# A Mamba layer with mixed inputs: sample mixing, step sizes and their series moved to other slots of a pass

## What is computed

```python
x = x + attn(cond(x, cond_128, ...))      # mixing of tokens, then a Mamba-2 layer
x = x + ffn(cond2(x, cond_128, ...))      # grouped convolution, then a gated dense layer

# cond: a small MLP on cond_128 gives 8 softmax weights per sample
agg_w = einsum('bk,koi->boi', att, weight); out = einsum('boi,bih->boh', agg_w, x) + agg_b
# attn: projection to gate, x, B, C and dt
conv = silu(causal 4-tap convolution of x, B, C)
dt_p = softplus(dt + dt_bias); dA = exp(dt_p * -exp(A_log))
state = state * dA + (dt_p * x) B;  y = state C + D x    # over the 32 tokens of a sample
y = rms_norm_by_group(y) * norm_weight * silu(gate);  out = y @ out_proj.T
```

## Time and profile before

| | us |
|---|---|
| median of 3 runs | 1548.5 (1547.95 to 1549.09) |
| the profiled execution | 1547.9 |
| its span in the trace | 1546.1 |
| TensorE busy | 1516.0 (98%) |
| VectorE busy | 1114.8 (72%) |
| ScalarE busy | 751.2 (49%) |
| GpSimd busy | 656.7 (42%) |

### The profile page before, as it was taken

The page is one execution under the profiler, slowest core; times in us unless marked ns, Lnnn a source line. Parts: engine busy times, 40 slices in busy tenths (PEclk is TensorE's granted clock), DMA queues, the critical chain, the costliest instruction groups (busy, mean ns, idle before and its releaser), DMA issues. The chain is left out here.

```text
span 1546.1 us, 31966 instructions
## 1 busy us (share of the span) xinstructions
PE 1516.0 (98%) x12839; PEld 1243.0 (80%) x12839; DVE 1114.8 (72%) x1725; ACT 751.2 (49%) x1302; POOL 656.7 (42%) x687
## 2 busy tenths in 40 slices
PE   8999999999999999999999999999999999999997
PEld 6778888888888888888877888888888888888687
DVE  6877767767777777777877767777777767777567
ACT  4654445454454445454564544545454544544442
POOL 4443544435253544434343352544434352543406
PEclk9999999999999999999999999999999999999999
DMA  6120212122120212111023221112121121113212
GB/s 221 60 71 23 83 35 69 56 57 67 49 66 18 81 37 69 55 56 55 9 68 124 56 69 49 52 31 77 42 69 55 56 69 48 50 32 102 93 37 109
DMA packets 57843, 97.71 MB, mean 63 GB/s; under 512 B 9120, under 2 KB 17824, under 8 KB 57696
## 3 DMA queue, kind: packets, MB, share of 16 engines
q1 hardware_dynamic: 57696, 95.67, 20.7%
HBM read 86.73 MB, written 8.91 MB: 62 GB/s over the span
## 5 line engine op out<-in xcount | busy, mean ns | idle before, releaser
L462 PE MATMUL PS<-xh,wh 128*128 128x512 f32 x1280 | 520.6, 407 | 0.7 <-DVE xl L967 0.6
L1041 DVE SCALAR_TENSOR_TENSOR cb<-PS,P,cb 128x496 f32<-128x496 f32 (+2 forms) x576 | 412.7, 717 | 128.8 <-ACT cb L772 115.0
L462 PE MATMUL PS<-xh,wl 128*128 128x512 f32 x1280 | 502.7, 393 | 0.0
L462 PE MATMUL PS<-xl,wh 128*128 128x512 f32 x1280 | 502.5, 393 | 0.0
L1343 POOL TENSOR_TENSOR wl<-rw,wh 128x512 fp32r<-128x512 f32 x160 | 206.1, 1293 | 221.4 <-ACT wh L717 207.5
L1353 POOL TENSOR_TENSOR ysum<-yq 128x256 f32<-128x256 f32 x128 | 112.6, 879 | 418.4 <-ACT yq L812 417.0
L462 PEld LDWEIGHTS PS<-xh,wl 128*128 128x128 f32 x1280 | 241.7, 189 | 52.6
L462 PEld LDWEIGHTS PS<-xh,wh 128*128 128x128 f32 x1280 | 242.1, 189 | 51.8 <-issue 1.3
L462 PEld LDWEIGHTS PS<-xl,wh 128*128 128x128 f32 x1280 | 242.1, 189 | 45.5
L772 ACT ACTIVATE cb<-PS,P 128x512 f32<-128x512 f32 x192 | 148.2, 772 | 179.4 <-PE PS L462 179.3
L560 PE MATMUL PS<-oh,yh 128*128 128x512 f32 x512 | 200.2, 391 | 2.5 <-issue 0.9
(11 more groups left out here) (189 smaller groups left out, 1861.2 us busy)
## 6 DMA issues: line engine op xcount, KB each, us to landing
rw<-in_w_in SPq DMA_DIRECT2D x160, 256.0 KB, 2.7
ro<-in_w_out SPq DMA_DIRECT2D x64, 256.0 KB, 3.1
dab<-rates SPq DMA_DIRECT2D x128, 128.0 KB, 3.2
x2s<-acc SPq DMA_DIRECT2D x16, 256.0 KB, 3.0
out_x<-acc SPq DMA_DIRECT2D x16, 256.0 KB, 2.5
acc<-in_x SPq DMA_DIRECT2D x3, 1024.0 KB, 10.1
wh<-x2s SPq DMA_DIRECT2D x8, 256.0 KB, 3.7
wl<-x2s SPq DMA_DIRECT2D x8, 256.0 KB, 4.6
```

Of the source, the lines that this page charges most:

```text
L462: mm = e.matmul(PS[:, proj_bank(n, m), :], w[:, m, 128 * k:128 * k + 128], v[:, k, a:a + 512], start=(i == 0), stop=(i == 11))
L1041: e.scalar_tensor_tensor(out=cv[:, :, d:32], in0=pv[:, :, 0:32 - d], scalar=P[:, P_CW + 4 * c + 3 - d:P_CW + 4 * c + 4 - d], in1=cv[:, :, ...
```

## The change

Mixing moves to slots 1 to 4 and `dt_product` to slot 5, now in bank PT for every block; it waits for `dt_summed` of the block before instead of for `scale_turned`. `dt_lower`, `dt_summed` and `dt_first` move to slot 6. Of the series of blocks 1 to 3, steps 0 to 4 run in VectorE's slot 8, steps 5 to 7 in slot 9, steps 8 to 11 in slot 4 of the next pass. The operands for mixing are made a slot or more earlier, those of tile 4 in front of the first taps. The wait for `dt_turn` of the block before moves from `dt_lower` to step 1 of the series, which overwrites `dr`; `turn_x`, second half, waits for `dt_summed` of this block, and Y no longer does. In pass 0, `G_all` moves to slot 4 and `G_mask` and the filling of `diag` to slot 5, `context` to slot 6, `side_inputs` to slot 9, GpSimd's mixing weights for tiles 12 to 15 from slot 4 to slot 3; `decays(0)` waits for `context`, since its output lies over that product's operand.

```diff
@@ -197,7 +197,7 @@
             return (SEG[0], PT, PY[1], PY[0])[i] if n == END else PO[i]
 
         def D_bank(b):
-            return PY[0] if b else PT
+            return PT
 
         def S_bank(n, i):
             return (PY[0] if i < 2 else SEG[0]) if n == END else PG
@@ -423,7 +423,7 @@
                 pe.wait_ge(wd_lo)
                 pe.wait_ge(x_lo, 4 * b + 3)
                 if b:
-                    pe.wait_ge(dtx_ok, ({1: 0, 2: 15, 3: 16}[b], 1))
+                    pe.wait_ge(d_sum, (b - 1, 1))
                 both = wds[:, :, :, :].rearrange("p k s c -> p k (s c)")
                 e.matmul(PS[:, D_bank(b), :], both[:, 0, :], xh[:, 0, a:a + 512], start=True, stop=False)
                 for k in range(4):
@@ -472,13 +472,11 @@
                     else:
                         pe.wait_ge(acc_ok, (n - 1, 3))
                 else:
-                    if n == 0:
-                        pe.wait_ge(d_sum, (0, 1))
-                    else:
+                    if n:
                         pe.wait_ge(dtx_ok, (n - 1, 3))
                         pe.wait_ge(acc_ok, (n - 1, 1))
-                    if n in BLOCK_AT and n >= 1:
-                        pe.wait_ge(x_lo, 4 * BLOCK_AT[n] + 3)
+                    if n in BLOCK_AT:
+                        pe.wait_ge(d_sum, (BLOCK_AT[n], 1))
                     if n in TURNED:
                         pe.wait_ge(dt_ok, TURNED[n])
                 for i in (0, 1):
@@ -510,8 +508,6 @@
                     pe.wait_ge(y_ok, (n, 1))
                 if i == 0:
                     pe.wait_ge(dtx_ok, (n, 1))
-                    if n in BLOCK_AT:
-                        pe.wait_ge(d_sum, (BLOCK_AT[n], 1))
                     if n >= 1:
                         pe.wait_ge(acc_ok, (n - 1, 3))
                     else:
@@ -576,25 +572,25 @@
                         dt_product(0)
                     if m == 6 and n in TURNED:
                         dt_turn(TURNED[n], n)
-                    if b is not None and 2 <= m <= 5:
-                        mix_tile(4 * b + m - 2, n)
-                    if m == 2:
-                        if n:
-                            Y(n - 1, 2)
-                            Y(n - 1, 3)
+                    if b is not None and 1 <= m <= 4:
+                        mix_tile(4 * b + m - 1, n)
+                    if n and m == 2:
+                        Y(n - 1, 2)
+                        Y(n - 1, 3)
+                    if m == (2 if n else 4):
                         G_all(n)
-                    if n == 0 and m == 5:
+                    if n == 0 and m == 6:
                         context()
                     if n and m in (1, 3, 4, 5):
                         i = (1, 3, 4, 5).index(m)
                         O(n - 1, i)
                         if i != 1:
                             S(n - 1, {0: (0,), 2: (1, 2), 3: (3,)}[i])
+                    if m == 5 and b is not None:
+                        dt_product(b)
                     if m == 7:
                         turn_x(n, 0)
                         turn_x(n, 1)
-                    if m == 8 and b is not None:
-                        dt_product(b)
                     if m == 9:
                         Y(n, 0)
                         Y(n, 1)
@@ -731,7 +727,6 @@
             def dt_lower(b):
                 act.wait_ge(D_ok, b)
                 if b >= 1:
-                    act.wait_ge(DT_ok, b - 1)
                     act.wait_ge(rate_out[b - 1], 1)
                 else:
                     act.wait_ge(mix, 2)
@@ -829,7 +824,7 @@
                         y_square(n - 1, 3)
                     if n == 0 and m == 1:
                         dt_lower(0)
-                    if b is not None and m == 9:
+                    if b is not None and m == 6:
                         dt_lower(b)
                     if m == 2:
                         silu(n, 1)
@@ -838,8 +833,6 @@
                     evac(n, m)
                     if n == 0 and m == 1:
                         dt_first(0)
-                    if b is not None and m == 9:
-                        dt_first(b)
                     if m == 6 and n in TURNED:
                         dt_turned(TURNED[n])
                     if n == 0 and m < 6:
@@ -848,6 +841,8 @@
                         silu(n, m - 1)
                     if n and m == 3:
                         y_high(n - 1, 3)
+                    if b is not None and m == 6:
+                        dt_first(b)
                     if m == 6:
                         scale_x(n, 0)
                         scale_x(n, 1)
@@ -857,8 +852,8 @@
                         split_o_hi(n // 2, m - 5)
                     if n % 2 == 1 and n < END:
                         split_w_hi(n // 2 + 1, m)
-                    if b is not None and 2 <= m <= 5:
-                        mixed_hi(4 * b + m - 2)
+                    if b is not None and 1 <= m <= 4:
+                        mixed_hi(4 * b + m - 1)
 
             def x3_biased(T):
                 act.wait_ge(conv_ok, T // 4)
@@ -996,6 +991,8 @@
                         if k == 11:
                             dve.wait_ge(rate_in, 1)
                         dve.wait_ge(d_step, (b, k - 1))
+                        if k == 1 and b:
+                            dve.wait_ge(DT_ok, b - 1)
                         if k == 1:
                             op = e.reciprocal(dr[:, :], da[:, :])
                         elif k == 2:
@@ -1021,6 +1018,7 @@
                 dve.wait_ge(ld_rate, n)
                 if n == 0:
                     dve.wait_ge(diag_ok)
+                    dve.wait_ge(cx_pe)
                 e.tensor_tensor_scan(Lt[:, :], dab[:, :], diag[:, :], 0.0, ALU.mult, ALU.max).then_inc(L_ok.sem, 1)
 
             def split_o_lo(u, j):
@@ -1115,18 +1113,19 @@
                 for m in range(10):
                     if n == 0 and m == 1:
                         dt_summed(0)
+                    if n == 0 and m == 0:
+                        mix_operands(4)
                     if n == 0 and m < 6:
                         taps(0, m)
                     if n == 0 and m == 0:
-                        mix_operands(4)
                         mix_operands(5)
                         mix_operands(6)
                     if n == 0 and m == 2:
                         mix_operands(7)
-                    if n >= 1 and n + 1 in BLOCK_AT and m in (6, 7):
-                        mix_operands(4 * BLOCK_AT[n + 1] + m - 6)
-                    if n and b is not None and m in (2, 4):
-                        mix_operands(4 * b + 1 + m // 2)
+                    if n >= 1 and n + 1 in BLOCK_AT and m in (6, 7, 9):
+                        mix_operands(4 * BLOCK_AT[n + 1] + {6: 0, 7: 1, 9: 2}[m])
+                    if n and b is not None and m == 3:
+                        mix_operands(4 * b + 3)
                     if n:
                         if m in (2, 5, 6):
                             variance(n - 1, {2: (0,), 5: (1, 2), 6: (3,)}[m])
@@ -1149,10 +1148,11 @@
                             add_out(n - 1, 2)
                         if m == 6:
                             add_out(n - 1, 3)
-                    elif m == 3:
+                    elif m == 5:
                         G_mask(n)
-                    if n == 0 and m == 6:
+                    if n == 0 and m == 9:
                         side_inputs()
+                    if n == 0 and m == 5:
                         e.tensor_copy(diag[:, :].rearrange("p (a t) -> p a t", a=32),
                                       bc(C[:, C_EQ:C_EQ + 32].rearrange("p (a t) -> p a t", a=1), 128, 32, 32)).then_inc(diag_ok.sem, 1)
                     if m == 7:
@@ -1162,18 +1162,20 @@
                         scale_turned(n, 1)
                         decayed(n, 0)
                         decayed(n, 1)
-                    if b is not None and m == 9:
+                    if b is not None and m == 6:
                         dt_summed(b)
                     if n and m < 6:
                         taps(n, m)
                     if n % 2 == 0 and m >= 6:
                         split_o_lo(n // 2, m - 6)
-                    if b is not None and 2 <= m <= 5:
-                        mixed_lo(4 * b + m - 2)
+                    if b is not None and 1 <= m <= 4:
+                        mixed_lo(4 * b + m - 1)
                     if n == 0 and 1 <= m <= 3:
                         dt_series(0, 4 * m - 4, 4 * m)
+                    if b is not None and m in (8, 9):
+                        dt_series(b, *((0, 5), (5, 8))[m - 8])
                     if n - 1 in BLOCK_AT and m == 4:
-                        dt_series(BLOCK_AT[n - 1], 0, 12)
+                        dt_series(BLOCK_AT[n - 1], 8, 12)
 
             def x3_low(T):
                 dve.wait_ge(x3_hi, T)
@@ -1385,12 +1387,12 @@
                         first_rates(TURNED[n])
                     if n == 0 and m < 6:
                         split_w_lo(0, m + 4)
```

(4 more changed lines are left out.)

## The result

The changed kernel takes 1555.2 us (median of 20 runs, 1553.7 to 1556.5) against 1549.5 for the kernel before in the same session: a ratio of 1.0039 (95% interval 1.0033 to 1.0046), 6.0 us slower by this ratio and 5.8 by the medians. The forecast was +2.1 us, 1550.6: right in sign, but inside what a measurement could tell from no change, and nearly 4 us short.

What follows compares the result with a forecast made beforehand. TensorE, busy 98%, bounds the kernel; only its waits and low clock, 21 us, can be won. Terms -9.9 - 2.1 + 6.5 + 4.7 + 2.9 = +2.1 us on 1548.5 gave 1550.6, range 1542.5 to 1555.5.

Steps and rivals of the forecast that it cites:

- term 3 of the series' end: Pass 0: GpSimd holding VectorE delays the first series by +1.7 us, between -3.8 and +4.4; series end forecast at 51.3.
- the mixing in pass 16: Pass 16: mixing one slot earlier puts each `mix_tile` closer behind its `mixed_lo`; cost taken as 0, at most 0.70 us.
- the first two: Pass 0, series end: one more `mixed_lo` less the mask, +0.3 us; idle time before `mixed_lo(4)`, +2.15 us.
- the −9.9: Passes 1 and 17: S waits (4.5 us), their low clock (3.4) and Y waits (2.0) all go.
- an earlier load: Passes 1 and 17: the scan of decays gets its load some 5 us earlier, so the Y waits (2.0 us) go.
- The O waits: New waits for late `y_out` and `y_low`: pass 1 +3.1 us plus 1.6 clock, pass 17 +2.1 plus 0.8.
- `dt_first` in front of the split: Before pass 17: `dt_first` with table load, 2.5 us in ScalarE's slot 6, delays `split_o_hi(8,1)`, then `decayed` and `y_out`.
- Pass 15, taken at nothing: Pass 15: steps moved to slots 8 and 9 cost 0; no output weights split, TensorE has 2 us of slack.
- The wait of `dt_product(3)` and the old O wait: Pass 16: both waits vanish, -1.2 us by the new bank and -0.9 by moving `dt_first` to slot 6.
- (a): Rival, faster: moved steps fit beside TensorE's last two projections, no O wait comes; -5.5 us, 1543.0; chance 0.23.
- (c): Rival, neutral: pass 0 costs little, series end near 49.5, O waits as forecast; +0.3 us, 1548.8; chance 0.13.
- (b): Rival, slower: GpSimd holding at +4.4 in pass 0, full low clock in pass 17; 1554.1 us; chance 0.22.

Runs made afterwards that it cites:

- pool_slot4: Changed kernel with GpSimd's mixing weights for tiles 12 to 15 back from slot 3 to slot 4; ratio 1.0013 to the kernel before.
- tile4_behind: Changed kernel with the operands of tile 4 made behind the first taps again; ratio 1.003 to the kernel before, median 1555.4 us.
- three_mended: Changed kernel with pool_slot4 and tile4_behind, plus series steps 0 to 2 in slot 8 and 3 to 11 in the next slot 4; ratio 0.999.
- passes_15_16_3_9: Kernel before with the change in passes 15 to 17 alone, series steps 0 to 2 in slot 8, 3 to 11 in slot 4; ratio 0.998.
- first_late: Changed kernel with `dt_first` behind `split_o_hi` in ScalarE's slot 6 instead of in front; ratio 1.0044 to the kernel before.
- pass_0: Kernel before with the change in pass 0 and for block 1 alone, passes 15 to 17 as before; ratio 1.0054.
- series_slot4: Changed kernel with all twelve series steps of blocks 1 to 3 back in slot 4 of the next pass; ratio 1.0046 to the kernel before.
- before_rates_first: Kernel before with `dab`'s load in front of the load of weights in SyncE's queue, nothing else; ratio 0.9984.
- mended_rates_first: three_mended with `dab`'s load in front of the load of weights in SyncE's queue; ratio 0.9959 to the kernel before, 1542.7 us.

## Why the prediction was right or wrong

The step that failed is the holding of VectorE by GpSimd. In pass 0 it was term 3 of the series' end, taken at +1.7 us and found at +4.1. In pass 15 it was no term at all, and the mixing in pass 16 that hangs on it was taken at 0 and found at +1.9.

**Pass 0: right mechanism, one term mis-sized.** The series ended at 54.42, and the program's first projection had started 0.55 later than before; so 53.9 against the 51.3 forecast. Of its three terms the first two hold: the idle time of 2.15 in front of `mixed_lo(4)` is there with 2.10. The third, the holding by GpSimd, was taken at +1.7. From the rows: steps 0 to 7 take 9.7 us after and 8.5 before (+1.2); the operands of tile 4 take 2.66 and those of tile 7 1.76, against 0.84 and 0.64 (+2.9). That is +4.1, and 47.12 + 0.3 + 2.15 + 4.1 = 53.7. I had listed both stretches of GpSimd and then took a value between the ends, on the argument that the order of the two engines is a race. It hardly is one: each long VectorE row here lies beside a row of GpSimd that had started first, and the step at 38.58 has its 2.44 in pool_slot4 again. With pool_slot4 and tile4_behind in one kernel (three_mended) the series ends 5.1 us earlier, counted from the first projection.

This is also where the Trainium skill ("SBUF — State Buffer", "Who interferes with whom") had pointed: a VectorE instruction with two SBUF inputs and a GpSimd one that reads SBUF shut each other out for the whole instruction. The trace agrees in size, +4.1 against the +4.4 of that reading. The step at line 1003 has a single tensor as input and was held too, 1.83 us against 0.28; the same section names `tensor_scalar` among the operations that can take the shared ports, and the trace agrees. The 1.22 us against 0.28 that the prediction gave for the rule on two inputs is such a `tensor_scalar` with a single tensor too, so it bore on this sentence of the section and not on that one.

From the end of the series on, the working held: 59.18 − 54.42 = 4.76 to the end of the split (4.8), then 77.60 − 59.24 = 18.36 to pass 1 (18.4). That TensorE would stand in pass 0 was right; that most of it shows earlier as well, at the operands of tile 7, I hadn't seen, and it costs nothing more, since VectorE's chain sets the end.

**Passes 1 and 17, what goes: right for S, by luck for Y.** The S and Y waits and their low clock are gone, the −9.9 are there: neither pass has such a row. The 5 us by which the scan was to be earlier are not: it still idles about 4 us for `dab`. TensorE doesn't feel it only because the O waits make it late. That the Y waits are gone is thus luck: the reason given, an earlier load, was wrong. The cover by O was not named, and by their profiles it is why three_mended and passes_15_16_3_9 won so little, until the load went first.

**The O waits: right.** 2.60 us in pass 1 (3.1 forecast) and 2.25 in pass 17 (2.1), released by `y_low`. Both were followed by a stretch at half the clock, where I had counted one in half the cases for pass 17: +0.9. Busy time by stretch, kernel after (columns of the earlier trace rows):

```profile
87.00:94.00 7.00, 7.00 (x63) 5.50 (x65) 5.66 (x9) 4.09 (x7) 5.06 (x6) 0.76 0.18 46
...
804.00:811.00 7.00, 7.00 (x85) 5.58 (x83) 5.47 (x10) 4.52 (x8) 4.97 (x5) 0.76 0.19 50
```

The kernel before has 1.00 in both stretches. The reason that I gave for the place of this wait in pass 17 (`dt_first` in front of the split) fell with first_late.

**Pass 15, taken at nothing: wrong.** The steps moved into slots 8 and 9 met GpSimd's weight splits there as well. VectorE after, end of pass 15:

```profile
736.96 1.38 DVE L987 TENSOR_SCALAR da<-pb 128x256 f32<-128x256 f32 x1
...
740.16 1.08 DVE L999 TENSOR_TENSOR da<-pb,dr 128x256 f32<-128x256 f32 x1
...
741.73 1.27 DVE L1003 TENSOR_SCALAR dr<-pb 128x256 f32<-128x256 f32 x1
742.92 1.38 DVE L950 TENSOR_TENSOR bd<-AW,C 128x128 f32<-128x128 f32 x1
...
745.68 0.68 DVE L1083 TENSOR_TENSOR y<-PS,big 128x512 f32<-128x512 f32 x1
```

Four of these instructions (736.96, 740.16, 741.73, 742.92) are 3.8 us over their twins of 0.28 to 0.42. `y_out` and `scale_turned` of the pass stand behind them, and TensorE's mixing in pass 16 waits 1.0 us for `scale_turned` and 0.9 us for a `mixed_lo` further on. In passes_15_16_3_9, with steps 3 to 7 out of the way, both waits are gone; no run moved GpSimd's splits of pass 15. I had priced the moved steps at their undisturbed length although and the earlier trace rows showed both lengths. The wait of `dt_product(3)` and the old O wait are gone, as forecast.

**The account** in us of the span, found minus forecast: pass 0 +2.6; O in pass 1 −0.4; S and Y −0.3; mixing in pass 16 +1.9; O and clock in pass 17 +1.0; start of the program +0.6; tail +1.1. Sum +6.5: 2.1 became 8.6. The last two belong to this execution; without them it is +6.9, against the +5.8 of the medians.

**The rivals.** (a), no O waits, and (c), a cheap pass 0, are out by their own signs. (b) came: series end past 52.3 and the full low clock, 1554.1 against 1555.2. That its number is so near is in part luck: it has no term for the mixing in pass 16 (+1.9), and the kernel before, measured beside the changed one, had a median 1.0 us above the 1548.5 that the sum started from. It had 0.22 and should have been the forecast: it needed nothing more than that rows already in view apply to the moved instructions too.

**Open.** Why the clock fell after some waits of 2 us and more and not after others is not settled. It fell after the two S waits of the kernel before (2.25 and 2.23) and the two O waits of the changed one. In pass_0 it stayed at 1.00 behind O (2.57) and S (2.25), in first_late behind O in pass 1 (2.59). That the spread of some kernels' times comes from the landing of the rates is argued from one profile of each kernel and was not tested by itself.

## What to carry to other kernels

An instruction moved to another slot must be priced at what it takes beside that slot's GpSimd work, not at its undisturbed length: find its twin that was held in the same trace and take that length wherever the two engines will run side by side. A wait that vanishes lets TensorE arrive earlier, so ask for each stretch what is late next; here it was one load behind a load of weights in SyncE's order, worth 4 us once nothing else covered it. And a full engine is not relieved by exchanging two of its instructions.

## What the runs showed of the hardware

Which instruction is held goes, in these rows, by where its operands lie. At 40.95 three taps that read PSUM took 2.21 us beside GpSimd's sums, as long as anywhere; the step at 38.58 and the operands at 43.41, with all inputs in SBUF, took 2.45 and 1.35 instead of 0.42 and 0.28.

In pass 16 the rates are stored by two transfers of 64 KB, and a load waits for them. From the end of the stores' row in SyncE's queue to the issue of that load 1.6 us passed in eleven of the fourteen profiles, but 1.9, 2.9 and 3.3 in passes_15_16_3_9, series_slot4 and before_rates_first (in the last one 3.2 in pass 17 too). The kernels in which TensorE waits for what hangs on such a load spread by 4.9 to 10.8 us from run to run (6 to 29 runs each), the others by 0.9 (mended_rates_first, 5 runs) to 3.3.
